# Two layer norms' factors in one GpSimd addition and one power, in the feed-forward of a one-core layer

## What is computed

```python
def _layernorm(x, axis=-1, eps=1e-05):
    m = jnp.mean(x, axis=axis, keepdims=True)
    v = jnp.var(x, axis=axis, keepdims=True)
    return (x - m) / jnp.sqrt(v + eps)

def fp4_linear(x, w):                      # fp4_quant_dequant: per block of 16, scale = max|x| / 6
    return jnp.einsum('bsk,nk->bsn', fp4_quant_dequant(x), fp4_quant_dequant(w))

x = _layernorm(x + attention(x))           # the first norm
h = silu(fp4_linear(x, w_gate)) * fp4_linear(x, w_up)
x = _layernorm(x + fp4_linear(h, w_down))  # the second norm
```

## Time and profile before

| | us |
|---|---|
| median of 3 runs | 1960.06 |
| lowest and highest | 1958.84, 1960.64 |
| the profiled execution, its own time | 1955.56 |
| its span, first to last instruction | 1953.8 |

### The profile page before, as it was taken

One profiled execution on the slowest core, in us unless ns is written; L12 is line 12 of the kernel. 1 busy time (PEld: TensorE's weight loads), 2 busy tenths in 40 slices (PEclk: granted clock), 3 DMA queues, 4 the chain that ended last, 5 costly groups with the idle time before them and its releaser, 6 DMA issues.

```text
span 1953.8 us, 43153 instructions
## 1 busy us (share of the span) xinstructions
PE 1921.8 (98%) x15934; PEld 1112.0 (57%) x15934; DVE 1828.5 (94%) x3084; ACT 1641.0 (84%) x3225; POOL 917.5 (47%) x779
## 2 busy tenths in 40 slices
PE   8999999999999999999999999999999999999998
PEld 7766444444444444444444444444478888888876
DVE  4798999999999999999999999998299999999997
ACT  6655999999999999999999999998867777777776
POOL 3000456674776665366122212212156666666785
PEclk9999999999999999999999999999999999999999
DMA  7885633454354445435444543542111111111210
GB/s 241 288 259 210 113 61 47 77 95 103 76 102 97 90 89 106 94 73 104 97 89 89 106 95 73 105 96 89 40 36 49 49 50 49 49 50 55 65 30 28
DMA packets 127200, 181.47 MB, mean 93 GB/s; under 512 B 37837, under 2 KB 82637, under 8 KB 126989
## 3 DMA queue, kind: packets, MB, share of 16 engines
q1 hardware_dynamic: 119308, 171.10, 37.4%
q10 hardware_dynamic: 7392, 7.34, 1.1%
q0 software_dynamic: 288, 0.27, 0.1%
HBM read 103.68 MB, written 73.40 MB: 91 GB/s over the span
## 4 chain that ended last, share of the span: by engine, by line
DVE 64%; PE 32%; issue 2%; DMA 1%; ACT 1%; SPq 0%; DVEq 0%; POOLq 0%; POOL 0%; ACTq 0%
DVE halfmax L1135 43%; DVE halfmax L1130 14%; PE ps L1411 10%; PE ps L1450 6%; PE ps L493 4%; PE ps L1399 2%; PE ps L505 2%; PE ps L1422 2%; PE ps L1045 2%; PE ps L1011 1%; PE ps L1458 1%; PE ps L480 1%; DVE room L1601 1%; PE ps L1467 1%; DVE room L1688 1%
## 5 line engine op out<-in xcount | busy, mean ns | idle before, releaser
L1096 ACT ACTIVATE room<-ps 128x512 f32<-128x512 f32 x2048 | 1086.3, 600 | 104.7 <-PE ps L1011 79.3
L1135 DVE TENSOR_REDUCE halfmax<-ps 128x1 f32<-128x512 f32 x1470 | 901.1, 677 | 0.0
L1011 PE MATMUL ps<-qs,ks 50*128 50x512 f32 x2048 | 719.0, 449 | 2.3 <-DVE halfmax L1135 1.2
L986 PE MATMUL ps<-ks,qs 48*128 48x512 f32 x1960 | 678.5, 439 | 4.5
L1045 PE MATMUL ps<-room,vals 128*17 128x256 f32 (+2 forms) x8192 | 578.1, 384 | 0.2 <-ACT craw L1104 0.2
L986 PEld LDWEIGHTS ps<-ks,qs 48*128 48x128 f32 x1960 | 311.4, 184 | 406.5 <-DVE halfmax L1135 250.5
L1011 PEld LDWEIGHTS ps<-qs,ks 50*128 50x128 f32 x2048 | 325.2, 184 | 19.9 <-ACT room L1096 14.6
L1045 PEld LDWEIGHTS ps<-room,vals 128*17 128x17 f32 x8192 | 167.4, 96 | 250.9 <-issue 186.8
L1130 DVE TENSOR_REDUCE halfmax<-ps 128x2 f32<-128x1024 f32 x245 | 296.1, 1209 | 1.2 <-PE ps L986 1.1
L164 POOL CAST mrow<-turned_rows 128x32 fp32r<-128x32 f32 x32 | 6.7, 208 | 589.7 <-DVE turned_rows L159 589.7
L1411 PE MATMUL ps<-wguT,xqT 128*128 128x512 f32 (+1 forms) x1152 | 266.7, 384 | 3.9 <-DVE xqT L1641 3.9
(11 more groups left out here) (120 smaller groups left out, 2264.3 us busy)
## 6 DMA issues: line engine op xcount, KB each, us to landing
qk_parts<-parts SPq DMA_DIRECT2D x64, 512.0 KB, 4.0
qs<-qk_parts SPq DMA_DIRECT2D x192, 128.0 KB, 4.3
ks<-qk_parts SPq DMA_DIRECT2D x192, 128.0 KB, 7.0
ctx_raw<-craw SPq DMA_DIRECT2D x64, 256.0 KB
ready<-passing SPq DMA_DIRECT2D x27, 512.0 KB, 4.2
pairs<-ready SPq DMA_DIRECT2D x27, 512.0 KB
out_dram<-fin SPq DMA_DIRECT2D x64, 128.0 KB, 1.8
xin<-in_L_attn_x_dram ACTq DMA_DIRECT2D x14, 512.0 KB, 5.5
```

Of the source, the lines that this page charges most:

```text
L986: nc.tensor.matmul(ps[:, MX + max_number(i, u, bank) % 4, :], qs[rows, i.slot(RING), pair, t * P:(t + 1) * P], ks[rows, i.slot(RING), pair ...
L1011: nc.tensor.matmul(ps[:, score_bank(i, s, n), :], ks[rows, slot, pair, kt * P:(kt + 1) * P], qs[rows, slot, pair, qh * BANK:(qh + 1) * BAN ...
L1096: nc.scalar.activation(prob[:, prob_slot(i, s), score_order(i, s)[n], :], ps[:, score_bank(i, s, n), :], ACT.Exp, scale=float(D) ** -0.5). ...
L1135: nc.vector.tensor_reduce(halfmax[:, i.slot(2), bank, column:column + 1], ps[:, at + bank, :], AX.X, ALU.max, negate=True).then_inc(max_re ...
```

## The change

The two GpSimd pairs of a step become one. At step k, the helper `power(k1, k2)` makes the first norm's factor of tile k - 1 and the second norm's factor of tile k - 8 in one addition over two columns and one power over two columns; the two slots of mv and rstd are reached with one strided slice. Tile k - 8 is one tile earlier than what step k's own second pair made (k - 7), so each second factor is made one step later, at the place of the first one's. Steps 1 to 7 have a first norm alone. Past step 64 there is no first norm left: at step 65 two single pairs stand one behind the other (tiles 57 and 58), and from step 66 each step makes tile k - 7's alone; all of them stand at the place of the first pair. The semaphores rstd1_ready and rstd2_ready become one, rstd_ready, and two tables, first_rstd and second_rstd, give the count to wait for. The diff, cut:

```diff
+    def norms(k):
+        if k <= NT:
+            return [(k - 1, k - 8 if k >= 8 else None)] if k >= 1 else []
+        return [(None, n) for n in (range(NT - 7, NT - 5) if k == NT + 1 else range(k - 7, min(k - 6, NT)))]
+
+    first_rstd, second_rstd = {}, {}
+    for count, (t1, t2) in enumerate((pair for k in range(TILES_RUN) for pair in norms(k)), 1):
+        if t1 is not None:
+            first_rstd[t1] = count
+        if t2 is not None:
+            second_rstd[t2] = count
...
         def output(t):
...
-            due(act, "rstd2_ready", t.lin(1, 1))
+            act.wait_ge(sems["rstd_ready"], second_rstd[t.k])
...
         def x1_normal(t):
-            due(act, "rstd1_ready", t.lin(1, 1))
+            act.wait_ge(sems["rstd_ready"], first_rstd[t.k])
...
-                due(dve, "rstd1_ready", t1.lin(1))
+                if t1.k > 0:
+                    dve.wait_ge(sems["rstd_ready"], first_rstd[t1.k - 1])
...
-            link = Chain(pool, sems[chain], 1, t)
-            link(nc.gpsimd.tensor_tensor(rstd[:, n, 0:1], mv[:, n, 1:2], numbers[:, 0:1], ALU.add))
-            nc.gpsimd.tensor_tensor(rstd[:, n, 1:2], rstd[:, n, 0:1], numbers[:, 1:2],
-                                    ALU.pow).then_inc(sems[name], 1)
...
+            n = [0] if k2 is None else [1 + k2 % 2] if k1 is None else [0, 1 + k2 % 2]
+            at = slice(n[0], n[-1] + 1, max(n[-1] - n[0], 1))
+            done[0] += 1
+            number = lambda c: numbers[:, c:c + 1].unsqueeze(2).to_broadcast([P, len(n), 1])
+            nc.gpsimd.tensor_tensor(rstd[:, at, 0:1], mv[:, at, 1:2], number(0), ALU.add).then_inc(sems["var_ready"], 1)
+            pool.wait_ge(sems["var_ready"], done[0])
+            nc.gpsimd.tensor_tensor(rstd[:, at, 1:2], rstd[:, at, 0:1], number(1),
+                                    ALU.pow).then_inc(sems["rstd_ready"], 1)
...
-            t = i.plus(-1)
-            if t.ok(NT):
-                due(pool, "mv1_ready", t.lin(1, 1))
-                due(pool, "x1_ready", t.lin(1))
-                power(t, 0, "pow1_chain", "rstd1_ready")
+            for k1, k2 in norms(i.k):
+                if k1 is not None:
+                    due(pool, "mv1_ready", k1 + 1)
+                    due(pool, "x1_ready", k1)
+                if k2 is not None:
+                    due(pool, "mv2_ready", k2 + 1)
+                    due(pool, "fin_ready", k2 - 1)
+                power(k1, k2)
...
-            t = i.plus(-7)
-            if t.ok(NT):
-                due(pool, "mv2_ready", t.lin(1, 1))
-                due(pool, "fin_ready", t.lin(1, -1))
-                power(t, second(t), "pow2_chain", "rstd2_ready")
```

More of the change, by code:

```diff
@@ L1320, in feed @@
     z = take(2, H)
-    names = ("xb_ready ctx_ready wo_psum wo_used mv1_ready rstd1_ready "
+    names = ("xb_ready ctx_ready wo_psum wo_used mv1_ready rstd_ready "
              "x1_ready xsum_ready xgrid_ready xq_ready xt_psum xqT_high xqT_ready xn_ready xm_ready xbend_ready hn_ready hm_ready hbend_ready gate_psum up_psum silu_ready h_made "
-             "hsum_ready hgrid_ready hq_ready hT_psum hT_ready dn_read dn_psum z_used mv2_ready rstd2_ready fin_ready "
-             "stats1_ready stats2_ready grid_chain pow1_chain pow2_chain shift1_chain shift2_chain last_ready").split()
+             "hsum_ready hgrid_ready hq_ready hT_psum hT_ready dn_read dn_psum z_used mv2_ready fin_ready "
+             "stats1_ready stats2_ready grid_chain var_ready shift1_chain shift2_chain last_ready").split()
     sems = {name: sem(name) for name in names}
@@ L1694, in vector @@
             if t7.k == NT - 1:
-                due(dve, "rstd2_ready", t7.lin(1, 1))
+                dve.wait_ge(sems["rstd_ready"], second_rstd[t7.k])
                 wait(dve, stored[t7.slot(2)], t7.turn(2, 16))
@@ L1700, in gpsimd, with power @@
     def gpsimd(pool, ks):
-        def power(t, n, chain, name):
-            link = Chain(pool, sems[chain], 1, t)
-            link(nc.gpsimd.tensor_tensor(rstd[:, n, 0:1], mv[:, n, 1:2], numbers[:, 0:1], ALU.add))
-            nc.gpsimd.tensor_tensor(rstd[:, n, 1:2], rstd[:, n, 0:1], numbers[:, 1:2],
-                                    ALU.pow).then_inc(sems[name], 1)
-            link.close()
+        done = [0]
+        def power(k1, k2):
+            n = [0] if k2 is None else [1 + k2 % 2] if k1 is None else [0, 1 + k2 % 2]
[6 more added lines that the diff above has]
+                                    ALU.pow).then_inc(sems["rstd_ready"], 1)
         for i in each(ks):
```

## The result

| | before | changed |
|---|---|---|
| median, us | 1959.17 (6 runs, 1958.76 to 1960.64) | 1966.25 (6 runs, 1964.55 to 1967.94) |
| ratio | | 1.0037 [1.0026, 1.0048] |
| profiled execution, span | 1955.56, 1953.8 | 1966.11, 1964.3 |
| mean granted clock of TensorE | 0.999 | 0.995 |

The change makes the kernel 0.37% slower, 7.1 us by the medians. The profiled execution of before lay 3.6 us under its median and that of the changed kernel at its own, so the spans differ by 10.5 us where the medians differ by 7. The profiles are therefore compared stretch by stretch. A single execution also differs from another in the phases ahead of the feed-forward, where all kernels here are the same: GpSimd's first factor starts between 1382.9 and 1389.2 us.

A forecast was written before the change was run, and what follows sets the result against it. Bounds: PE in the steady stretch, DVE (locked with GpSimd) in steps 54 to 63, a chain through all engines at the end. 1.2 + 2.9 = +4.1 us on 1960.06 gave 1964.2, range 1959.2 to 1967.8.

The forecast's parts named there:

- rival C: Power's second column costs 0.3 us or more, using up DVE's slack in the steady stretch: +7.5, 1967.6 us; chance 0.13.
- Removed pairs worth 0: On GpSimd, 57 of 128 pairs go, 46 us of its time, but it idled there: worth 0.
- The power's second column, 0.16 us: In the GpSimd pair, the power's second column adds 0.16 us, taken from a power of 32 columns.
- Rival A: The power's second column is free, so its 1.6 us in steps 54 to 63 would be nothing; chance 0.14.
- the bound of 0.36: Upper bound for the power's second column: all that the power takes over the addition, 0.55 - 0.19 us.
- Steady stretch, 0: From 1412 to 1823 us, DVE is 0.16 us later each step against 0.26 of slack: 0.
- Limit at 0.35 us and the turning of the order at L1608: In the steady step, xq starts before DVE's L1608 (hn + hm) only while delayed up to 0.35 us.
- Steps 54 to 63, +1.2: DVE sets the step: +1.6 us from the longer power, -0.4 at step 54; the 0.54 us stall stays.
- rival B: Stall of steps 55 to 63 goes, step falls from 8.60 to 8.20: 1959.4 us, chance 0.10; best case 1955.5, 0.05.
- End, +2.9: From step 65, second-norm pairs stand ahead of work PE waits for: +2.9 us, the middle of 2.3 and 3.6.
- Signs named beforehand: Expected trace signs, among them L1481 of tile 63 waiting 1.8 us and GpSimd waiting at steps 65 and 66.
- Rival D: At the end, what the change delays had slack, so no lengthening there: +1.2, 1961.3 us; chance 0.06.

The follow-up runs named there:

- e6: e1 with the power made over four columns, each factor computed twice; 1961.45 against 1958.89 us before, 1.0016.
- e5: e1 with the double pair split into two single pairs at the same place, first norm's first; 1962.62 against 1958.89 us before, 1.0021.
- e4: e1 plus one wait: in steps 54 to 63 L1737's addition waits for xn; 1953.86 against 1958.89 us before, repeated 1954.12 against 1957.95.
- e1: Changed kernel with the old order at its end, second norm's pairs behind xq, hg and hq; 1960.03 against 1958.41 us before, 1.0006.
- e2: Kernel before with only the new order at its end, no pair merged; 1964.79 against 1958.41 us before, 1.0033.
- e3: Changed kernel with identity transposes keeping TensorE busy through the waits at the end; 1962.09 against 1958.41 us before, 1.0018.
- e0: The changed kernel run again, beside the kernel before on the same chip; 1965.17 against 1958.41 us, 1.0035.
- e7: e4 with two single pairs at the head of the step instead of the merged one, second norm's first; 1955.65 against 1958.89 us before, 0.9986.

## Why the prediction was right, and where it was not

- **Direction, time and range**: 1964.2 forecast, 1959.2 to 1967.8; measured 1966.25. Against before it was +4.1, and is +7.1 and +6.8. The direction was right for the reasons given, but that the time lies inside the range is in part luck: the upper bound was set by rival C, whose cause did not occur in the changed kernel, and it happened to leave room for a loss of some 3 us that the prediction did not have at all (the clock, below). The band that it held likeliest, within 0.2% at 0.49, did not come; slower by over 0.2% had 0.46.
- **Removed pairs worth 0**: right. GpSimd is busy 22 us less in the steady stretch and no time comes of it.
- **The power's second column, 0.16 us**: right. L1727 takes 0.89, the forecast behind L1664; e6 confirms the slope. Rival A, a free second column, by which the 1.6 us of this term would be nothing, is refuted, and rival C (0.3 us or more) as well. The addition's 0.19 us, on which the bound of 0.36 rests, is not among; the trace of before has it (L1704 at 1846.36).
- **Steady stretch, 0**: right in each quantity: hn + hm 1.18, DVE's wait 0.2, PE without a gap.
- **Limit at 0.35 us and the turning of the order at L1608**: right, by e5 and e6. Past it the steady step is 0.04 us longer in both: the exhaustion of DVE's slack that rival C reckoned with, in kernels that delay xq further than the change does.
- **Steps 54 to 63, +1.2**: measured 1.24, step 8.77 for 8.76. The stall stayed and rival B is refuted. Which operation it hits was left open; it is xn, L1737 having the port first. For rival B I had missed only that it was one wait away: with e4's line it happens, at 8.22 us a step.
- **End, +2.9**: the step that failed by size. The order gives 3.6, the upper of the two bounds: hg gets the port ahead of L1593 (L1593 lasts 1.57 us). I had taken the middle of two cases of which only one can happen, when the two requests were forecast 0.01 us apart (hg starts 0.01 ahead of L1593 in the trace). The rest, some 3.3 us, is a term that the sum did not have: the waits that the order adds on PE are followed by matmuls at the half clock. The trace of before has waits of PE of 1.16 us at most there, and its ten matmuls take 2.32 and 2.40 us; the sum shifted PE's work and left its durations as they were, in a stretch with waits of 2 us before them. e1, e2 and e3 show both parts.
- **Signs named beforehand**: PE's L1481 of tile 63 waits 1.97 us, of which 1.8 were forecast as delay, and GpSimd waits for L1708 at steps 65 and 66, ahead of hg. Rival D (the end hidden) is refuted.

With the sizes of the first trace the sum would have been 1.2 + 3.6 + 3.3 = 8.1 against 7.1 and 6.8 measured by medians (the repeat's trace has less of the clock's part, 2.7 by e0 less e3); and e1's +1.6 stands for the 1.2 of steps 54 to 63.

**What stays open.** That the end's low clock belongs to the added waits is shown (it is there in the changed kernel, e0 and e2, and absent in e1 and e3). Why it is now one group of matmuls and now another, and once none behind the first wait, is not, and neither is the low clock in the fill of two executions. e7 stands 1.0 to 1.8 us above e4 (by ratios and medians), within the intervals; the traces show 0.4 to 0.5 of that, so no more is shown for the double pair's own worth in e4.

## What to carry to other kernels

Work saved on an engine that idles gave nothing here. What gave 4 us was the place of the two products in the steps: the first early enough to be done before xn, the second told to wait for xn; and most of that came without the saving (e7). An engine that shows as busy throughout can still have lost time: count the steps in a stretch as well (e5). A step that is moved ahead in a loop must be read again for the loop's end, where what it waits for comes last and all behind it on its queue waits too. And where a change adds idle time to TensorE, price it once as time and, as a risk, once more as the clock of the matmuls behind it, with the durations of a trace that has such waits.

## What the runs showed of the hardware

- **The wait costs twice.** Of the six waits of PE of about 2 us at the end (1.97 and 2.02, in the changed kernel, e0 and e2), five are followed by ten matmuls in 3.3 to 3.9 us instead of 2.32 to 2.40, with a granted clock between 0.50 and 0.85 over the stretches of 5 us that hold most of each; behind the sixth (e0's first) they take 2.32. In e0 and e2 the last group, with no such wait before it, is slow as well (3.60 and 3.44). With identity transposes in the waits they take 2.32 and 2.40. In this case that was about 3 of 7 us.
- **The port goes to whoever asks first, and 0.16 us decide.** In e4 the addition starts 0.16 us behind hn and waits for hn's whole length; in the changed kernel it is ahead of xn by 0.03 and xn waits for it. The Trainium skill has this in SBUF — State Buffer, Who interferes with whom: the pair of ports that DVE's second SBUF input shares with GpSimd is an exclusive lock, and the order of issue decides who blocks. The traces agree. One and the same pair in both orders: with xq first, xq takes 0.62 us and hn + hm 1.18 (the changed kernel); with hn + hm first, that takes 0.88 and xq 0.92 (e5). The addition takes 0.72 us when it is first and 1.32 behind hn.
- **A GpSimd power costs by the column**: 0.55 us for one (free of DVE), about 0.16 for each further, measured at 2, 4 and 32 columns; an addition of one or two columns costs 0.28 us in the steady step either way.
